# Counting a graph's edges with narrower windows of destinations, and some one-hots moved to VectorE

## The reference

```python
dst = jnp.minimum((3125 * jax.random.uniform(..., (100000,)) ** 2.0).astype(jnp.int32), 99999)
_o = jnp.argsort(dst, stable=True)
src = src[_o]; dst = dst[_o]
...
edge_index = jnp.stack([src, dst])
x = _layernorm(x + _L0_gnn_ref(x, ..., edge_index))                  # GCN, degree-normalized
x = _layernorm(x + _L1_gnn_ref(x, edge_index, ...))                  # sum over neighbours
x = _layernorm(x + _L2_gnn_ref(edge_index, edge_type_100, x, ...))   # two CompGCN layers, by edge type
x = _layernorm(x + _L3_gnn_ref(x, ..., src, dst))                    # GCN, both degrees
```

## Time and profile before

| | us |
|---|---|
| median of 3 runs | 3369.73 (3368.91 to 3371.75) |
| the profiled execution | 3372.2 |
| its span in the profile | 3370.4 |
| POOL busy | 2289.2 (68%) |
| PE busy | 2028.9 (60%) |
| DVE busy | 1973.2 (59%) |
| ACT busy | 1359.1 (40%) |
| the sends, line 260, 784 of them | 775.3 busy, 360.2 idle before |
| layer 2's gathers, line 1412, 1568 of them | 1512.0 busy, 546.5 idle before |

### The profile page before, as it was taken

How to read it: one execution, slowest core, us unless ns; L and a number is a source line. 1 busy time by engine, 2 the same in 40 slices (tenths; PEclk the granted TensorE clock), 3 DMA queues, 4 the chain that set the end, 5 groups by cost and what they waited for, 6 DMA issues and landing times.

```text
span 3370.4 us, 43753 instructions
## 1 busy us (share of the span) xinstructions
PE 2028.9 (60%) x12073; PEld 1554.8 (46%) x12074; DVE 1973.2 (59%) x5137; ACT 1359.1 (40%) x3329; POOL 2289.2 (68%) x2359
## 2 busy tenths in 40 slices
PE   0028788775857186555665555556656566666557
PEld 0014444433424175555555555445555555555544
DVE  7849999971232254444444444557666667666663
ACT  3237777740121064333443333244333344333322
POOL 0677777777677677777777777277777777777700
PEclk9995666657977555555555555667777777677768
DMA  1000000005911132222222222153322323333271
GB/s 37 1 1 2 2 2 2 2 2 88 158 8 21 28 75 56 53 54 53 52 54 54 53 53 47 39 133 85 76 76 77 79 74 82 79 77 77 62 164 42
DMA packets 182981, 183.50 MB, mean 54 GB/s; under 512 B 78966, under 2 KB 155746, under 8 KB 181987
## 3 DMA queue, kind: packets, MB, share of 16 engines
q1 hardware_dynamic: 107313, 101.77, 14.5%
q0 software_dynamic: 75424, 78.83, 10.2%
HBM read 153.48 MB, written 26.94 MB: 54 GB/s over the span
## 4 chain that ended last, share of the span: by engine, by line
POOL 64%; issue 22%; DVE 6%; PE 4%; DMA 2%; DVEq 1%; SPq 0%; ACT 0%; POOLq 0%; ACTq 0%; PEldq 0%
POOL adj_again_middle L1412 41%; POOL sorted_edges L260 23%; DVE acc L1489 1%; PE psum L1037 1%; DMA adj_again_middle<-gather_table,gidx_s 1%; DVE adj_again_middle L1507 1%; DVE runs L393 1%; DMA l_v<-in_L_gnn_beta 1%; PE psum L1034 1%; PE psum L1956 0%; DVE picked L364 0%; DVE rank L402 0%; PE psum L1945 0%; PE psum L2257 0%; PE psum L1880 0%
## 5 line engine op out<-in xcount | busy, mean ns | idle before, releaser
L1412 POOL DMA_INDIRECT adj_again_middle<-gather_table,gidx_s x1568 | 1512.0, 964 | 546.5 <-issue 475.0
L260 POOL DMA_INDIRECT sorted_edges<-rec,row_i x784 | 775.3, 989 | 360.2 <-issue 266.2
L1450 ACT ACTIVATE adj_again_middle<-cst,lo_s 128x125 f32<-128x125 f32 x1664 | 527.1, 388 | 1074.3 <-PE psum L1562 1070.6
L1536 PE MATMUL psum<-rel_parts,oh_t 128*128 128x96 bf16 (+1 forms) x4704 | 548.0, 294 | 611.9 <-DVE oh_t L1475 313.8
L1562 PE MATMUL psum<-adj_again_middle,oh_s 128*125 x3328 | 725.5, 391 | 133.6 <-DVEq L1490 123.2
L1536 PEld LDWEIGHTS psum<-rel_parts,oh_t 128*128 128x128 bf16 x4704 | 451.0, 131 | 688.6 <-DVE oh_t L1475 344.8
L1562 PEld LDWEIGHTS psum<-adj_again_middle,oh_s 128*125 128x125 f32 x3328 | 666.3, 298 | 166.7 <-issue 163.7
L1507 DVE TENSOR_TENSOR adj_again_middle<-adj_again_middle,psum 128x256 f32<-128x256 f32 (+1 forms) x784 | 399.3, 550 | 560.1 <-DMA adj_again_middle<-gather_table,gidx_s 508.5
L1489 DVE TENSOR_TENSOR acc<-acc,psum 125x64 f32 (+1 forms) x1664 | 419.3, 252 | 295.5 <-issue 96.9
L651 PE MATMUL psum<-oh_dst,oh_src 128*125 128x500 bf16 x784 | 408.8, 595 | 99.2 <-DVE oh_dst L607 80.9
L1454 ACT ACTIVATE oh_s<-adj_again_middle,cst 128x500 f32<-128x500 f32 x416 | 296.1, 712 | 13.6
(11 more groups left out here) (371 smaller groups left out, 1090.2 us busy)
## 6 DMA issues: line engine op xcount, KB each, us to landing
tb<-sorted_types SPq DMA_DIRECT2D x392, 128.0 KB, 3.2
adj_again_middle<-gather_table,gidx_s POOLq DMA_INDIRECT x1568, 2.6
adj_saved<-adj SPq DMA_DIRECT2D x6, 2734.4 KB
sorted_edges<-rec,row_i POOLq DMA_INDIRECT x784
adj_again_middle<-adj_saved SPq DMA_DIRECT2D x3, 2734.4 KB
adj_again_last<-adj_saved SPq DMA_DIRECT2D x2, 2734.4 KB
adj_again_first<-adj_saved SPq DMA_DIRECT2D x1, 2734.4 KB
gather_table<-scaled SPq DMA_DIRECT2D x12, 224.0 KB
```

Of the source, the lines that this page charges most:

```text
L260: nc.gpsimd.indirect_dma_start(rec_d[c // HC], bass.IndirectOffsetOnAxis(ap=row_i[:, c:c + 1], axis=0), rec[:, c, :], None).then_inc(sent. ...
L1412: nc.gpsimd.indirect_dma_start(gx[g % DEEP][:, k, :], None, table_d[d], bass.IndirectOffsetOnAxis(ap=gidx_s[:, t:t + 1], axis=0),).then_in ...
L1450: sq = nc.scalar.activation(sq_s[:, k, :], iota[:, 0:LO], ACT.Square, bias=lo_s[:, t:t + 1], scale=-1.0)
L1536: mm = nc.tensor.matmul(ps_rel[g % RELS_KEPT][:, k * RS:k * RS + W], oh_t[g % (AHEAD + 1)][:, k * P:(k + 1) * P], rel_parts[:, s, :], star ...
```

## The change

Three edits of the count, and what they need in the sort:

1. **Narrower windows.** The destinations counted for a pair are 12, 12, 17 or 20, by the quarter of the 392 pairs. The one-hots, the products and the adds of a pair shrink from 500 to 300, 300, 425 or 500 columns. `too_wide` compares each pair with its own window.
2. **Quads in the first quarter.** The 98 pairs of the first quarter are taken two at a time: four tiles add into one bank, and VectorE adds that bank once. Both pairs of a quad use the quad's first destination as base, which takes three small operations in the sort. The adds fall from 392 to 49 + 294 = 343.
3. **Every seventh source one-hot by VectorE.** Quads 3, 10, 17, ... (28 of 196) are made by one `is_equal` of VectorE over [128, 500] in place of ScalarE's four squares and one relu.

```diff
+QUARTER_PAIRS = PAIRS // 4
+WINDOWS = (12, 12, 17, WIN)
+VECTOR_QUADS = frozenset(range(3, NQ, 7))
+def pair_window(n):
+    return WINDOWS[n // QUARTER_PAIRS]
+UNITS = [(n, n + 1) for n in range(0, QUARTER_PAIRS, 2)] + [(n,) for n in range(QUARTER_PAIRS, PAIRS)]
...
                     link(v.tensor_scalar(pair_base[:], ends[:, 0, :, :], float(PITCH - WIN), None, ALU.min))
+                    link(v.tensor_reduce(quad_first[:], pair_base[:, 0, :], AX.X, ALU.min))
+                    link(v.tensor_scalar(past_it[:, 0, :], pair_base[:, 0, :], quad_first[:], by_quad, ALU.subtract, ALU.mult))
+                    link(v.tensor_tensor(pair_base[:, 0, :], pair_base[:, 0, :], past_it[:, 0, :], ALU.subtract))
                     link(v.tensor_tensor(past_it[:], ends[:, 1, :, :], pair_base[:], ALU.subtract))
+                    link(v.tensor_tensor(past_it[:], past_it[:], window_of..., ALU.is_ge))
                     link(v.tensor_reduce(too_wide[:], past_it[:], AX.XY, ALU.max))
-                    link(v.tensor_scalar(too_wide[:], too_wide[:], float(WIN), None, ALU.is_ge))
...
+                    def make_sources(q):
+                        if q >= SRC_RING:
+                            dve.wait_ge(counted.sem, batches(2 * (q - SRC_RING) + 2))
+                        v.tensor_tensor(oh_src[q % SRC_RING][:], iota..., nat_lo[quad q]..., ALU.is_equal
+                                        ).then_inc(src_made_here.sem, 1)
...
+                            if n % 2 == 0 and n // 2 in VECTOR_QUADS:
+                                make_sources(n // 2)
...
-                                ins = v.tensor_scalar(oh_dst[n % DST_RING][:, k, :], iota16[:],
+                                ins = v.tensor_scalar(oh_dst[n % DST_RING][:, k, 0:pair_window(n) * BLOCKS],
+                                                      iota16[:, 0:pair_window(n) * BLOCKS],
...
-                        if n >= BANKS_USED:
-                            pe.wait_ge(added.sem, n - BANKS_USED + 1)
+                        if begins and unit >= BANKS_USED:
+                            pe.wait_ge(added.sem, unit - BANKS_USED + 1)
...
-                                             start=(k == 0), stop=(k == 1), skip_group_check=True)
+                                             start=(begins and k == 0), stop=(ends_ and k == 1), skip_group_check=True)
```

More of the change, by code:

```diff
@@ L73 @@
 assert SPANS - TILES <= KEPT - 3 * GROUP and (HS - HT) % GROUP == 0 and HT % GROUP == 0
+def pair_window(n):
+    return WINDOWS[n // QUARTER_PAIRS]
+UNITS = [(n, n + 1) for n in range(0, QUARTER_PAIRS, 2)] + [(n,) for n in range(QUARTER_PAIRS, PAIRS)]
+UNIT_OF = {n: u for u, pairs in enumerate(UNITS) for n in pairs}
 def dft(d):
@@ L103, in constants @@
     c[:, 3 * P + 8 + BLOCKS:3 * P + 8 + BLOCKS + NQ] = np.arange(NQ) + 1
+    c[:, 3 * P + 4] = q < QUADS // 2
+    c[0:QUADS, 3 * P + 5:3 * P + 7] = [[pair_window(2 * (h * QUADS + i)) for h in range(2)] for i in range(QUADS)]
     c[:, -2] = q * WIN
@@ L288, in gnn_stack @@
             past_it = sb("past_it", [QUADS, 2, 2], F32, sort)
+            quad_first = sb("quad_first", [QUADS, 1], F32, sort)
             too_wide = sb("too_wide", [QUADS, 1], F32, sort)
@@ L566, in _, with squares @@
                 def _(act):
-                    def squares(q):
+                    mine = [q for q in range(NQ) if q not in VECTOR_QUADS]
+                    def squares(i):
+                        q = mine[i]
                         for k in range(QUAD):
-                            sq = nc.scalar.activation(sq_src[q % 2][:, k, :], iota[:, 0:LO], ACT.Square,
+                            sq = nc.scalar.activation(sq_src[i % 2][:, k, :], iota[:, 0:LO], ACT.Square,
                                                       bias=nat_lo[:, q * QUAD + k:q * QUAD + k + 1], scale=-1.0)
@@ L572, in _ @@
                     squares(0)
[L573 to L577, removed]
+                    for i, q in enumerate(mine):
+                        if i + 1 < len(mine):
+                            if i >= 1:
+                                act.wait_ge(src_made.sem, i)
+                            squares(i + 1)
                         if q >= SRC_RING:
                             act.wait_ge(counted.sem, batches(2 * (q - SRC_RING) + 2))
[L580 to L581 removed]
+                        act.wait_ge(src_squared.sem, i + 1)
+                        nc.scalar.activation(oh_src[q % SRC_RING][:], sq_src[i % 2][:], ACT.Relu,
                                              bias=one_col, scale=-2.0).then_inc(src_made.sem, 1)
@@ L591, in load_bases, with add_unit @@
                         return [dve.snap(r, min_val=0, max_val=PITCH - WIN) for r in regs]
-                    for n in range(PAIRS + PAST):
+                    def add_unit(u, bases):
+                        first, last = UNITS[u][0], UNITS[u][-1]
+                        wide_ = pair_window(first)
+                        dve.wait_ge(counted.sem, batches(last + 1))
+                        if u >= 1:
+                            dve.wait_ge(added.sem, u)
+                        to = adj_by_node[:, :, bass.ds(bases[first % AT_ONCE], wide_)]
+                        v.tensor_tensor(to, to, psum[0:LO, pair_bank(u):pair_bank(u) + wide_ * BLOCKS].rearrange("p (n s) -> p s n", s=BLOCKS),
+                                        ALU.add).then_inc(added.sem, 1)
+                    def make_sources(q):
+                        if q >= SRC_RING:
+                            dve.wait_ge(counted.sem, batches(2 * (q - SRC_RING) + 2))
+                        v.tensor_tensor(oh_src[q % SRC_RING][:],
+                                        iota[:, 0:LO].rearrange("p (a l) -> p a l", a=1).to_broadcast([P, QUAD, LO]),
+                                        nat_lo[:, q * QUAD:(q + 1) * QUAD].rearrange("p (t a) -> p t a", a=1).to_broadcast([P, QUAD, LO]),
+                                        ALU.is_equal).then_inc(src_made_here.sem, 1)
+                    units_added = 0
+                    for n in range(PAIRS + 1):
                         if n < PAIRS:
@@ L644, in _ @@
                         if n % 2 == 0:
-                            pe.wait_ge(src_made.sem, q + 1)
-                        if n >= BANKS_USED:
-                            pe.wait_ge(added.sem, n - BANKS_USED + 1)
+                            if q in VECTOR_QUADS:
+                                pe.wait_ge(src_made_here.sem, sum(k <= q for k in VECTOR_QUADS))
+                            else:
+                                pe.wait_ge(src_made.sem, sum(k not in VECTOR_QUADS for k in range(q + 1)))
+                        unit = UNIT_OF[n]
+                        begins, ends_ = n == UNITS[unit][0], n == UNITS[unit][-1]
+                        if begins and unit >= BANKS_USED:
+                            pe.wait_ge(added.sem, unit - BANKS_USED + 1)
                         pe.wait_ge(dst_made.sem, n + 1)
+                        wc = pair_window(n) * BLOCKS
                         for k in range(2):
                             of = oh_src[q % SRC_RING][:, first + k, :]
-                            nc.tensor.matmul(psum[0:LO, pair_bank(n):pair_bank(n) + WC], of, oh_dst[n % DST_RING][:, k, :],
-                                             start=(k == 0), stop=(k == 1), skip_group_check=True)
+                            nc.tensor.matmul(psum[0:LO, pair_bank(unit):pair_bank(unit) + wc], of, oh_dst[n % DST_RING][:, k, 0:wc],
+                                             start=(begins and k == 0), stop=(ends_ and k == 1), skip_group_check=True)
                             mm = nc.tensor.matmul(psum[0:LO, deg_bank + h * BLOCKS:deg_bank + (h + 1) * BLOCKS], of,
```

25 lines of the change are left out of this document (12 added, 13 removed).

## The result

The change takes **3365.98 us** where the kernel before takes 3371.72 (medians of 20 runs each), a ratio of **0.9981**, 95% interval 0.9975 to 0.9988: about 6 us faster, where 3371 and no change were forecast.

The account below looks back on a forecast made before the run. POOL's queue of sends was taken to bound the kernel, hiding the 78 us shorter count; collisions of +1.6 us and 0 for other terms gave 3371.3 us against the 3369.73 median, likeliest no change, range 3361 to 3380.

Parts of the forecast that it names:

- The bound and the slack: POOL's sends bound the end; VectorE's 57.29 us idle time before the last sends' records hides any change of the count.
- The start of the count: Count's start stays fixed by POOL's constant at 221.56; added sort operations cost under 1 us inside 42 us idle.
- The length of the count: Four quarters of 80, 97, 122 and 134 us plus 8 give 441 against 519.7: about 78 us shorter, bounds 50 and 105.
- the term for the ends: Start of the count and its last adds: 8 us, as before, added to the four quarters.
- the lockstep of the third quarter: Pairs of 425 columns may fall into step with POOL at 1.26 us; up to 30 us more, half taken: 15.
- The long stop: POOL's 12.67 us stop at 838, taken for a code load queued behind the matrix saving, likeliest still meets it: 0 us.
- a rival with 14%: Count ends 97 to 116 us earlier, so the stop near 838 escapes the matrix saving: -9.4, with collisions -7.8, 3362; 14%.
- The collisions: Sends in the count delayed by VectorE's one-hots: 8.3 us against 6.7, so +1.6 us, bounds -6.7 and +18.
- The source one-hots: 28 made by VectorE at 0.62 us each in the first half; cost to sends 0 to 0.6 us, taken as 0.
- The rule on two SBUF inputs: Skill's rule: VectorE operations with two SBUF inputs contend with GpSimd instructions reading SBUF; at most 9 us, set aside.
- rival 4: One-hots of 425 columns lose the fast form: 43 us more VectorE, count only 35 us shorter, still 3371; within no change.
- The sum: Send delays over the whole kernel sum to +1.6 us: 3371.3 against the median, likeliest no change, 70%.

Follow-up runs that it names:

- the second chip: The unedited changed kernel measured again on another chip against the kernel before: 3362.76 us against 3369.35, ratio 0.9983.
- the run with narrow windows: Changed kernel with windows of 10, 10, 15 and 19 destinations and no clears, against the kernel before: 3367.91 us, ratio 0.9997.

## Why the prediction was wrong, point by point

- *The bound and the slack.* Right. POOL is the chain, the count and layers 0 and 1 are covered, and VectorE's idle time grew from 57 to 148 us (forecast 135). 40 us more work in the kernel before did not lengthen it.
- *The start of the count.* Right: 222.34 in place of 222.71.
- *The length of the count.* This is **the step that failed**: 441 us forecast, 420.4 measured. The first one-hot of the second, third and fourth quarters, and the last add:

```profile
303.13 1.17 DVE L654 TENSOR_SCALAR oh_dst<-iota,x 128x300 bf16<-128x300 int16 x4
...
396.27 0.56 DVE L654 TENSOR_SCALAR oh_dst<-iota,x 128x425 bf16<-128x425 int16 x2
...
508.87 0.62 DVE L654 TENSOR_SCALAR oh_dst<-iota,x 128x500 bf16<-128x500 int16 x2
...
642.04 0.68 DVE L625 TENSOR_TENSOR adj<-adj,psum 125x500 f32 x1 [0.20 <-DVE adj L625]
```

The first quarter took 80.0 us (303.13 less 223.14, forecast 80), the second 93.1 (97), the third **112.6** (122), the fourth with the last adds 133.8 (134 and 8 for both ends). The first block one-hot adds 0.8. ScalarE bound the first quarter as forecast, busy for 78.67 of its 80 us:

```profile
223.10:303.10 80.00, 65.69 (x384) 57.51 (x384) 71.05 (x257) 78.67 (x212) 58.18 (x59) 0.66 0.02 2
```

Of the 20.6 us, 9.4 are the third quarter's and 7.4 the term for the ends. That term was counted twice: the fourth quarter's 1.33 a pair is 519.70 / 392, and the 519.70 hold the start and the last adds already. The second quarter gives 3.9: its collisions, 10 us in the forecast, hardly came, while the pairs themselves were slower than the forecast's 0.75 us, 0.80 at the median, since a one-hot of 300 columns takes 0.21 from start to start and not 0.155. The term that was mis-sized most is the lockstep of the third quarter, 15 us. It did not form:

```profile
440.18 0.56 DVE L654 TENSOR_SCALAR oh_dst<-iota,x 128x425 bf16<-128x425 int16 x2
...
441.17 0.74 DVE L654 TENSOR_SCALAR oh_dst<-iota,x 128x425 bf16<-128x425 int16 x2
...
442.33 0.61 DVE L654 TENSOR_SCALAR oh_dst<-iota,x 128x425 bf16<-128x425 int16 x2
```

A pair takes 0.99, then 1.16, and not 1.26 again and again. Of the 97 spacings of that quarter none lies between 1.24 and 1.30 us; in the kernel before 54 do. The bare sum without collisions had been 107, and 5.6 us were added to it, not 15. So the saving moved by 101 us (806.67 to 705.49) where 78 were forecast, and 97 was the point from which the stop escapes.

- *The long stop.* The mechanism was right: the saving delays it, and its cost is 9.7 us (12.67 less 2.97; forecast 9.4). What it is was wrong (a count of sends, not code), and so was "about 116 sends each time": 113 sends and the stop itself fill the 148 us. For the time that made no difference. It was weighed as a rival with 14% because the count's length was taken as known to some 10 us. Its two bounds, 50 and 105, held 101, and held the window of 97 to 116 only in part; I should have given it a third. That the stop escaped is luck all the same: nobody placed the saving, and it was over 7 us ahead of the stop in the profile.
- *The collisions.* The sum came out right: 313.52 less 318 x 0.959 is 8.5 us in the count, forecast 8.3, before 6.7. The layers' sends cost 258.82 less 260 x 0.959, 9.5 us, before 9.6. But it holds 3 us of the next point, which was put at 0, so the released collisions were dearer in the forecast than in the trace, and the two errors cancel. In four other profiles of the changed count the 784 sends took 778.7 to 780.4 us, 2 to 4 us more than in this one. Taking turns is what the trace shows, but not for the whole of a send: in the kernel before, one-hots that start 0.05 to 0.35 us after a send's start take their plain 0.34 us, and those that start 0.55 after it 0.50.
- *The source one-hots* took 0.675 us each, forecast 0.62:

```profile
L632 DVE TENSOR_TENSOR oh_src<-cst,x 128x500 bf16<-128x500 f32 x28 | 18.9, 675 | 0.0
```

Their cost to the sends was put at 0, and this is a second term that was wrong. A send that starts while one runs is held:

```profile
515.22 0.67 DVE L632 TENSOR_TENSOR oh_src<-cst,x 128x500 bf16<-128x500 f32 x1
515.22 1.49 POOL L276 DMA_INDIRECT sorted_edges<-rec,row_i  x1 [0.30 <-issue]
```

It takes 1.49 us in place of 0.96. One that starts 0.16 us after its one-hot takes 1.34, one at 0.29 takes 1.21, one at 0.47 takes 1.03: the hold ends about 0.54 us after the start of the one-hot. A block one-hot of 700 columns does the same (368.94, 0.15 us after its start: 1.54 us). The 38 sends that overlap a source one-hot took 1.046 us on average, 3.3 us together over 0.959; in the five profiles with the change's windows it is 2.7 to 3.3 us. Three that start within 0.02 us of the one-hot's start were not held. The row from which the forecast took 0 was a send that began 0.73 us into a block one-hot of 0.88, too late to be held for long. The rule on two SBUF inputs that the prediction set aside points the right way, at a third of its bound of 9 us.

- *The odd width* (rival 4) kept the fast form: the one-hots of a pair of 425 columns start 0.24 us apart (median), and two of them with their add fit into 0.99 us above; a pair of 500 columns has 0.26. The Trainium skill's "VectorE: DVE Perf Modes", mode 2x_2P, allows odd sizes that are equal on both sides, and here the trace agrees with its 0.24 us.
- *The sum.* +1.6 - 9.7 is -8.1, against -7.5 in the profiled spans and -5.7 in the medians; the same two kernels differ by 6.6 us in the medians of the second chip. Why the medians show less stays open. The busier sends of the other profiles are part of it, and in some runs the saving may have ended late enough to touch the stop.

## What to carry to other kernels

When an edit works beside the bound, its gain or loss is decided by what it moves, so list the large transfers that shift with it and the events on the critical engine that they may meet, and give each a window of shifts rather than one number. If the window's edge lies inside the error of the length that was estimated, the chance belongs to the window, not to the middle value. A saving or load that can be placed freely is better placed on purpose, between two such events: 40 us of idle waiting in front of it brought as much as the whole change.

## What the hardware showed that I had not expected

- This stream of indirect DMAs from POOL stops after every 113, for 2.96 to 3.5 us in 66 of the 84 stops, 4.1 to 4.5 when a packet of an instruction queue starts with it, 5.1 and 5.3 beside the loads ahead of layer 0, and 9.7 to 12.7 when it meets the saving. 80 more instructions ahead of it do not move that.
- A stop that begins 4 us after the saving's start already has its full length (12.70, and 12.60 in the run with narrow windows), while one that begins 7 us after its last issue has 2.97.
- A send of POOL that starts during a VectorE `is_equal` of two SBUF tiles waits for most of what is left of it: up to 0.53 us with 128x500 (1.49 against 0.96).
- Two engines can fall into step: pairs of 500 columns at 1.27 us with POOL's 1.26, though VectorE takes 1.11 where no send holds it. At 425 columns, with 0.99, they did not.
